# Top-2 experts computed on tokens that are sorted by expert on the chip

## What is computed

```python
def reference(x, Wq, Wk, Wv, w_gate, w_in, w_out):
    xn = _layernorm(x, axis=-1)
    # attention: Q, K, V = (xn @ W.T).reshape(H, b, s, 16)
    #   out = softmax(Q K^T) V, y = out + xn, normalised over each batch entry
    logits = xn @ w_gate.T
    top_logits, top_idx = jax.lax.top_k(logits, 2)
    top_gates = softmax(top_logits)
    gates = (one_hot(top_idx, 8) * top_gates[..., None]).sum(axis=1)
    for e in range(8):
        y = y + gates[:, e:e + 1] * ((xn @ w_in[e].T) @ w_out[e].T)
    return x + attention + y
```

## Time and profile before

| | us |
|---|---|
| median of 3 runs | 1054.75 |
| lowest, highest | 1052.57, 1057.66 |
| the profiled execution | 1050.42 |
| its span in the trace | 1048.6 |
| busy: TensorE, VectorE, ScalarE, GpSimd | 1007.0, 875.9, 627.5, 78.4 |

### The profile page before, as it was taken

One profiled execution on the slowest core, in us unless ns is written; L12 is line 12 of the kernel. 1 busy time (PEld: TensorE's weight loads), 2 busy tenths in 40 slices (PEclk: granted clock), 3 DMA queues, 4 the chain that ended last, 5 costly groups with the idle time before them and its releaser, 6 DMA issues.

```text
span 1048.6 us, 20711 instructions
## 1 busy us (share of the span) xinstructions
PE 1007.0 (96%) x7816; PEld 524.0 (50%) x7816; DVE 875.9 (84%) x1255; ACT 627.5 (60%) x1231; POOL 78.4 (7%) x205
## 2 busy tenths in 40 slices
PE   6698999999999999999999999999999999999995
PEld 6476788888885433333333333333333333333332
DVE  4331678787768999999999999999999999999976
ACT  2120011211110288888888888888888888888885
POOL 2100011001100000000000000000000000010001
PEclk9899999999999899999999999999999999999998
DMA  9588346545555012222222222222222222222204
GB/s 349 212 290 265 101 107 170 151 122 165 145 147 159 5 54 73 60 72 58 72 60 72 60 70 62 70 62 68 64 68 64 63 69 64 68 61 70 61 27 161
DMA packets 127042, 108.58 MB, mean 104 GB/s; under 512 B 81120, under 2 KB 102368, under 8 KB 126944
## 3 DMA queue, kind: packets, MB, share of 16 engines
q1 hardware_dynamic: 114016, 86.03, 28.9%
q10 hardware_dynamic: 12928, 21.24, 6.0%
HBM read 80.75 MB, written 42.21 MB: 117 GB/s over the span
## 4 chain that ended last, share of the span: by engine, by line
PE 89%; DVE 6%; issue 1%; DMA 1%; ACT 1%; ACTq 1%; POOL 0%; SPq 0%; POOLq 0%; DVEq 0%
PE ps L921 27%; PE ps L903 22%; PE ps L856 15%; PE ps L891 11%; PE ps L819 5%; PE ps L792 3%; PE ps L807 2%; PE ps L932 2%; DVE negm L628 1%; PE ps L944 1%; DVE acc L616 1%; PE ps L780 1%; ACTq L443 1%; DVE spare L560 1%; ACT stage L440 1%
## 5 line engine op out<-in xcount | busy, mean ns | idle before, releaser
L628 DVE TENSOR_REDUCE negm<-ps 128x1 f32<-128x1024 f32 x512 | 619.0, 1222 | 30.4 <-PE ps L891 12.1
L472 ACT ACTIVATE wp<-ps 128x512 f32<-128x512 f32 x684 | 369.4, 603 | 87.3 <-PE ps L903 60.1
L903 PE MATMUL ps<-qf,kf 50*128 50x512 f32 x1024 | 388.6, 456 | 1.9 <-DVE ps L696 1.7
L891 PE MATMUL ps<-kf,qf 48*128 48x512 f32 x1024 | 368.2, 450 | 0.2 <-DVE negm L628 0.2
L903 PEld LDWEIGHTS ps<-qf,kf 50*128 50x128 f32 x1024 | 160.0, 186 | 206.4 <-ACT wp L472 107.3
L921 PE MATMUL ps<-wp,vb 128*17 128x256 f32 x2736 | 215.4, 387 | 0.3 <-issue 0.3
L891 PEld LDWEIGHTS ps<-kf,qf 48*128 48x128 f32 x1024 | 145.9, 186 | 7.4 <-issue 5.7
L472 ACT ACTIVATE vstage<-ps 128x512 f32<-128x512 f32 x170 | 102.4, 602 | 24.9 <-PE ps L903 11.2
L856 PE MATMUL ps<-mth,xth 128*128 128x512 f32 x256 | 103.8, 405 | 3.4 <-DVE spare L560 2.5
L921 PEld LDWEIGHTS ps<-wp,vb 128*17 128x17 f32 x2736 | 46.9, 95 | 119.1 <-ACT wp L472 45.9
L472 ACT ACTIVATE picks<-ps 128x512 f32<-128x512 f32 x170 | 102.6, 603 | 0.0
(11 more groups left out here) (106 smaller groups left out, 724.0 us busy)
## 6 DMA issues: line engine op xcount, KB each, us to landing
feat_d<-qk_d SPq DMA_DIRECT2D x64, 256.0 KB, 4.4
qf<-feat_d SPq DMA_DIRECT2D x128, 128.0 KB
qk_d<-stage ACTq DMA_DIRECT2D x32, 256.0 KB
qk_d<-spare ACTq DMA_DIRECT2D x32, 256.0 KB
qf<-feat_d SPq DMA_DIRECT2D x128, 64.0 KB
kf<-feat_d SPq DMA_DIRECT2D x128, 64.0 KB
v_d<-vstage ACTq DMA_DIRECT2D x8, 544.0 KB, 4.9
vb<-v_d SPq DMA_DIRECT2D x128, 34.0 KB, 2.6
```

Of the source, the lines that this page charges most:

```text
L472: nc.scalar.activation(weight_tile(n, j, b)[:, h * HALF:(h + 1) * HALF], ps[:, ST_BANK[(2 * unit + b) % 3], :], ACT.Exp).then_inc(exp_done, 1)
L628: nc.vector.tensor_reduce(negm[:, n % 2, qt:qt + 1], ps[:, b:b + 2, :].rearrange("p b c -> p (b c)"), AX.X, ALU.max, negate=True).then_inc ...
L891: last = nc.tensor.matmul(ps[:, MAX_BANK[turn % 2] + half, :], qf[rows, u, qt * P:(qt + 1) * P], kf[rows, u, :], start=True, stop=True)
L903: nc.tensor.matmul(ps[:, ST_BANK[(2 * unit + half) % 3], :], kf[rows, u, j * P:(j + 1) * P], qf[rows, u, h * HALF:(h + 1) * HALF], start=T ...
```

## The change

Each token is computed with its two experts only. The 32 tiles are two parts of 16 (`PARTS`, `PT`). VectorE counts the choices (`count_choices`), TensorE makes running counts over partitions (`rank_choices`, three small matmuls), and VectorE works out at which tile each expert's tokens start (`start_tiles`), the row of each token and choice (`place_choices`) and the expert of each of 40 tiles (`name_owners`). GpSimd scatters the layernormed tokens by indirect DMAs of 128 rows into a table in HBM (`xs_d`), which SP has cleared whole by one plain DMA for each part. The sorted table has room for 40 tiles a part (each expert's rows filled up to a tile), so 80 tiles or 20 blocks of four are computed whatever the choices. A block is loaded (`sorted_tokens`), transposed, split and multiplied (`expert_tile`): high and low half of the expert's matrix stand side by side in `mm`, so the four matmuls give high x both (512 columns) and low x high (256), twice. The expert's number is read from registers. ScalarE copies the second half of the bank (`expert_out`), VectorE adds the first (`add_halves`), SP stores the block (`expert_rows`). In stage C GpSimd gathers each token's two rows, weights and adds them (`gather`, `combine`).

What moves with it: the projections of chunks 2 to 7 stand alone before the sorted products; the first 16 score maxima stand behind blocks 4 to 19; 48 of the 64 regroups move into stage C; weights have three slots, since `xn` is written by the layernorm itself; the layernorms of stage A are earlier.

```diff
+    AHEAD = 16
+    PARTS = 2
+    PT = NT // PARTS
+    MOST = PT * P // P
+    TILES = -(-((2 * PT * P + E * (P - 1)) // P) // TC) * TC
+    MB = TILES // TC
+    NMB = PARTS * MB
+    PACK = 8
+    WORDS = TILES // PACK
+    WARM = NMB - 2 * NKT
...
+    xs_d = [nc.dram_tensor(f"xs_d{i}", [TILES * P, D], FP32, kind="Internal").ap() for i in range(PARTS)]
+    ys_d = [nc.dram_tensor(f"ys_d{i}", [TILES * P, D], FP32, kind="Internal").ap() for i in range(PARTS)]
...
-        room = [wp[:, i, :] for i in range(4)] + [xn[:, TC * c:TC * (c + 1), :].rearrange("p t d -> p (t d)") for c in range(NC // 2, NC)]
+        room = [wp[:, i, :] for i in range(4)] + [xnc[:, i].rearrange("p t d -> p (t d)") for i in range(2)]
         win = [r.rearrange("p (h d) -> p h d", h=HU) for r in room[0::2]]
         wout = [r.rearrange("p (h d) -> p h d", h=HU) for r in room[1::2]]
         WS = len(win)
...
+                i = 2 * e + s
+                slot, earlier = i % WS, i - WS
                 if earlier >= 0:
-                    sp.wait_ge(*((m_ready, KT * (earlier + 1)) if s else (half_done, earlier + 1)))
+                    sp.wait_ge(*((m_ready, KT * (earlier // 2 + 1)) if earlier % 2 else (half_done, earlier // 2 + 1)))
...
+            sp.wait_ge(att_const, 2)
+            for part in range(PARTS):
+                sp.dma_start(xs_d[part].rearrange("(p r s) d -> p r (s d)", p=P, s=2),
+                             ot[:].rearrange("p g b t -> p (g b t)")[:, 0:2 * D].unsqueeze(1).to_broadcast([P, TILES // 2, 2 * D])
+                             ).then_inc(cleared[part], 16)
...
+            def sorted_tokens(b):
+                if b >= 2:
+                    sp.wait_ge(xt_psum, KT * (NC + b - 1))
+                if b % MB == 0:
+                    sp.wait_ge(scattered[b // MB], 16 * 2 * PT)
+                sp.dma_start(xnc[:, b % 2], xs_d[b // MB][b % MB * CH:(b % MB + 1) * CH].rearrange("(t p) d -> p t d", p=P)).then_inc(xs_in[b % 2], 16)
+
+            def expert_rows(b):
+                sp.wait_ge(moe_added, TC * (b + 1))
+                sp.dma_start(ys_d[b // MB][b % MB * CH:(b % MB + 1) * CH].rearrange("(t p) d -> p t d", p=P), outs[b % 4]).then_inc(ys_out[b % 4], 16)
+
+            sp.wait_ge(m_ready, KT * E)
+            sorted_tokens(0)
+            sorted_tokens(1)
+            for b in range(NMB):
+                if b >= 1 and b + 1 < NMB:
+                    sorted_tokens(b + 1)
+                if b == NMB - 2:
+                    max_rows(0)
+                expert_rows(b)
 
             for n in range(NB - 1):
                 if n:
                     sp.wait_ge(pv_done, NKT * n)
                 values(n + 1)
                 max_rows(n + 1)
+                if n + AHEAD < NB:
+                    regroup(n + AHEAD)
...
+            for part in range(PARTS):
+                pool.wait_ge(cleared[part], 16)
+                for k in range(2):
+                    pool.wait_ge(placed, 2 * part + k + 1)
+                    for t in range(PT * part, PT * (part + 1)):
+                        nc.gpsimd.indirect_dma_start(
+                            out=xs_d[part], out_offset=bass.IndirectOffsetOnAxis(ap=placeu[:, k, t:t + 1], axis=0),
+                            in_=xn[:, t, :], in_offset=None).then_inc(scattered[part], 16)
+            def gather(t):
+                part = t // PT
+                if t == 0:
+                    pool.wait_ge(xt_psum, KT * (NC + NMB))
+                if t % PT == 0:
+                    for i in range(4):
+                        pool.wait_ge(ys_out[i], 16 * len(range(i, MB * (part + 1), 4)))
+                for k in range(2):
+                    nc.gpsimd.indirect_dma_start(
+                        out=xnc[:, t % 2, k, :], out_offset=None, in_=ys_d[part],
+                        in_offset=bass.IndirectOffsetOnAxis(ap=placeu[:, k, t:t + 1], axis=0)).then_inc(gathered[t % 2], 16)
+
+            def combine(t):
+                rows = xnc[:, t % 2, 0:2]
+                pool.wait_ge(gathered[t % 2], 32 * (t // 2 + 1))
+                nc.gpsimd.tensor_tensor(rows, rows, gates[:, t, :].unsqueeze(2).to_broadcast([P, 2, D]), ALU.mult
+                                        ).then_inc(weighted, 1)
+                pool.wait_ge(weighted, 2 * t + 1)
+                nc.gpsimd.tensor_tensor(xnc[:, t % 2, 0], xnc[:, t % 2, 0], xnc[:, t % 2, 1], ALU.add).then_inc(weighted, 1)
+                pool.wait_ge(weighted, 2 * t + 2)
+                nc.gpsimd.tensor_tensor(acc[:, t, :], acc[:, t, :], xnc[:, t % 2, 0], ALU.add).then_inc(acc_done, 1)
...
+            for n in range(NB):
                 if n % 2 == 0 and n >= 4:
                     residual(n // 2 - 2)
                 max_halves(n)
+                if n % 2:
+                    gather(n // 2)
+                elif n:
+                    combine(n // 2 - 1)
+            combine(NT - 1)
...
+            xt_out(2)
             for c in range(2, NC):
-                xt_out(c)
                 v_out(c)
-                second_weight(c)
+                if c + 1 < NC:
+                    xt_out(c + 1)
+                if c > 2:
+                    second_weight(c - 1)
                 qk_out(c)
+            second_weight(NC - 1)
+
+            def expert_out(i):
+                b, t = divmod(i, TC)
+                if b >= 4 and t == 0:
+                    act.wait_ge(ys_out[b % 4], 16 * (b // 4))
+                act.wait_ge(moe_ready, i + 1)
+                nc.scalar.copy(outs[b % 4][:, t, :], ps[:, Y_BANK[i % 4], D:2 * D]).then_inc(moe_half, 1)
+
+            xt_out(NC)
+            for half in range(2):
+                act.wait_ge(qk_stored[half], 64 * NC)
+            for i in range(PARTS * TILES):
+                expert_out(i)
+                if i % TC == 0 and i + TC < PARTS * TILES:
+                    xt_out(NC + i // TC + 1)
+            act.wait_ge(named, PARTS)
...
+            def count_choices(c):
+                rows, own = slice(TC * c, TC * (c + 1)), TC * c % PT
+                g(nc.vector.tensor_tensor(occ[:, own:own + TC], oh1[:, rows], oh2[:, rows], ALU.add))
+                for t in range(own, own + TC):
+                    dve.wait_ge(summed, TC * c + t - own)
+                    nc.vector.tensor_tensor(before[:, t + 1], before[:, t], occ[:, t], ALU.add).then_inc(summed, 1)
...
+            def place_choices(part):
+                rows = slice(PT * part, PT * (part + 1))
+                own = work[:, 0:PT * E].rearrange("p (t e) -> p t e", e=E)
+                for k, onehot in enumerate((oh1, oh2)):
+                    g(nc.vector.tensor_tensor(own, place, onehot[:, rows], ALU.mult))
+                    g(nc.vector.reduce_sum(placef, own, AX.X))
+                    nc.vector.tensor_scalar(placeu[:, k, rows], placef, float(P), None, ALU.mult).then_inc(placed, 1)
+                    dve.wait_ge(placed, 2 * part + k + 1)
...
+            def add_halves(i):
+                b, t = divmod(i, TC)
+                dve.wait_ge(moe_half, i + 1)
+                nc.vector.tensor_tensor(outs[b % 4][:, t, :], ps[:, Y_BANK[i % 4], 0:D], outs[b % 4][:, t, :], ALU.add
+                                        ).then_inc(moe_added, 1)
...
             m_lo(0)
-            dve.wait_ge(const_step, 6 + E)
+            layernorm(1)
+            dve.wait_ge(const_step, CONSTS)
+            dve.wait_ge(ones_done, 2)
             choose_experts(0)
             m_lo(1)
             dve.wait_ge(w_lo, 2)
             qk_lo_halves(0, range(4))
+            lo_halves(1)
             gate_weights(0)
-            layernorm(1)
-            lo_halves(1)
+            count_choices(0)
...
+            lo_halves(2)
+            layernorm(NC - 1)
+            for c in range(2, NC):
+                if c > 2:
+                    choose_experts(c - 1)
+                    count_choices(c - 1)
+                if c + 1 < NC:
+                    lo_halves(c + 1)
+                if c == NC // PARTS:
+                    start_tiles(0)
+                qk_lo_halves(c, range(2))
+                if c == NC // PARTS:
+                    place_choices(0)
+                qk_lo_halves(c, range(2, 4))
+                if c > 2:
+                    gate_weights(c - 1)
+                if c == NC // PARTS + 1:
+                    name_owners(0)
+
+            choose_experts(NC - 1)
+            count_choices(NC - 1)
+            gate_weights(NC - 1)
+            start_tiles(1)
+            place_choices(1)
+            name_owners(1)
+            lo_halves(NC)
+            for i in range(PARTS * TILES):
+                add_halves(i)
+                if i % TC == 0 and i + TC < PARTS * TILES:
+                    lo_halves(NC + i // TC + 1)
+                if i == PARTS * TILES - 1:
+                    dve.wait_ge(moe_added, PARTS * TILES)
                     nc.vector.memset(ps[:, PV_BANK, 0:POS // 4 + P], 0.0).then_inc(att_const, 1)
-                maxima(n, qt)
-                if n == 1 and qt == 1:
```

(42 more changed lines are left out.)

274 lines of the change are left out of this document (132 added, 142 removed).

## The result

The changed kernel takes **1195.76 us** (1192.38 to 1199.79) where the one before, run beside it, takes 1054.4 us: a ratio of 1.134, 95% interval 1.129 to 1.138. The profiled execution has a span of 1193.0 us. Forecast was 1102 us, range 1060 to 1145: the sign was right, the size not. The loss against the kernel before is 141 us where some 50 were forecast.

What follows compares the result with a forecast made beforehand. TensorE was taken to bound the expert stage alone, and attention with ScalarE and VectorE close behind. Profiled 1050.4 us, plus 50 for a later first attention score, plus 2 in attention, gave 1102 us; range 1060 to 1145.

Steps and rivals of the forecast that it cites:

- Stage A: Weights and expert matrices, before the first token-by-expert product: end forecast at 96 us (94 to 106) instead of 105.65.
- Projections at 12.9 us a chunk, ScalarE's pace: Chunks 2 to 7 without dense products as cover: ScalarE's copies and DMA issues set 12.9 us each, 77 for six.
- only the stores of a chunk must land within its round: Bare projections: the argument against DMA saturation, whose cost was put at 4 us more per chunk.
- 112 us of work in 108 us of time: DMA from about 90 us on: clearings, stores, scatter, regroups and features, lasting until 202 us or later.
- saturation rival: Bare projections: chunk stores land late, each of six chunks takes 4 us longer, 1126 us in all; chance 0.13.
- VectorE's list after the last projection: Before the first sorted tile: 48 small operations and two low halves, 13 us uncovered on TensorE; tile at 198 us.
- GpSimd's writes: Scatter into the sorted table: 32 issues at 1.3 us from about 142 us, done at 184, so not late.
- Blocks at 10.8 us: Sorted experts: each block of four tiles holds one whole DMA trip, 10.8 us (8.5 to 13.2).
- half of 3.0 us: Sorted blocks: transposes and three tiles at 1.2 GHz would cost 3.0 us more; 1.5 us was taken.
- Attention +2: Attention stage: regroups and gathers hidden, but more traffic beside the row maxima's transfer, 2 us longer (0 to 30).
- The sign: Whole kernel: slower than before, with chance 0.88.
- the blocks' load trip: Sorted blocks: next load issued only behind the previous block's store, landing in 4.7 us (3.9 to 5.4), exposed each block.

Runs made afterwards that it cites:

- the ladder: Chunks 2 to 7, one thing added per step: forecast 72.5 us, stores and work alone 76.2, attention's preparation 94.3, clearings 111.6, indirect writes 129.4.
- x3: Changed kernel without GpSimd's indirect writes and without the two table clearings, blocks loading the input instead: 1141.8 us.
- x4: Changed kernel with each sorted block's load issued one block earlier, ahead of a store: 1096.0 us, ratio 1.042 to the kernel before.
- x12: x4 with spaced indirect writes, regroupings paced or moved behind blocks, features ahead of the first block, maxima's rows first in attention: 1075.6 us, ratio 1.020.
- x6: x4 with a GpSimd memset of 1024 columns ahead of each indirect write, to space them: 1087.5 us, ratio 1.029.

## Why the prediction was wrong

- **Stage A**: right in its direction. The last product of two weights ended at 92.4 us, below the bounds of 94 to 106, and the first value product came 4.7 us earlier than forecast. The gap ahead of expert 5's products, which was to grow from 3.87 us to 5.3, fell to 2.58.
- **Projections at 12.9 us a chunk, ScalarE's pace**: this step failed: 57 us over, of which 5 were kept in hand for DMA (198 to 203) and 4.7 came back from stage A; the rest is the 48 us of the first tile. By the ladder the 57 are 4 for the work and the stores themselves, 18 for the attention's preparation, 17 for the clearings and 18 for the indirect writes. ScalarE's own terms nearly hold when it is alone (13.8 to 15.4 us a chunk), but one of them, 0.59 us for the issue of a store, was too small here: the 40 issues of chunks 2 to 6 took 37.2 us instead of 24. The wait that I let off with "only the stores of a chunk must land within its round" is what failed: they didn't land within it, and one was waited for 17.3 us. DMA was priced by bytes, as 112 us of work in 108 us of time; x3 shows a store waited for while only 2.1 of sixteen engines are busy, which a price by bytes over all of them can't hold. The saturation rival had the place and the mechanism, and sized it at 24 us; it was 35 by the two steps of the ladder.
- **VectorE's list after the last projection**: right; from the last chunk's first value copy to the first tile 25.5 us, forecast 12.9 + 13.
- **GpSimd's writes**: 1.3 us each was right (1.27), their end at 184 near (192.3, from 151.8 instead of 142). What failed is that I asked only when they end and put what they do to others at nothing: 39 us in all, 12 by traffic, 27 by form, 13 of them ahead of the first tile and 25 in the first blocks. No row of before could show it, and none of the rivals had it.
- **Blocks at 10.8 us**: right, 11.2. The loads landed in 4.7 us as taken. Of the clock I had taken half of 3.0 us; the transposes took 1.97 us in every block, where 0.87 is the length at the full clock, and the three tiles 2.5 to 3.9 instead of 2.1; together that is 2.2 us over the full clock in the mean. By that the Trainium skill, "TensorE: Matmul & The Clock Gate", section "HAM oscillation", which lets every round of such a loop start at the low clock, was nearer than my half. 18 x 0.4 = 7 us; the other 25 of the 33 us lost in the blocks are the second stall.
- **Attention +2**: measured +13.8, inside its bounds of 0 to 30. The cause I named, more traffic beside the row maxima, was it, and mis-sized: 11.5 us are the reads.
- **The sign**: the blocks' load trip, which was to decide it, is there and cost 94 us. But slower would have come out without it too: x4, where the trip is hidden, is still 42 us over before, by the terms that I had wrong.

**Left open**: why ScalarE's waits for TensorE take so long beside dense indirect writes, even where the work waited for was done before. The runs show that both form and density are needed, not the mechanism; the trace puts part of the waits down to an unknown queue and the others to nothing that it sees. Loading of code hardly explains it: from 150 to 200 us the profile has three packets of the instruction queues, 0.3% of the DMA engines' time.

## What to carry to other kernels

When a long TensorE phase is removed, its cover goes for every transfer that stood beside it: price each store that gates a buffer with all that is queued in its stretch, ask how many of the DMA engines each transfer keeps busy and not only its bytes, and ask what total is left. Issue the load of the next round ahead of the store of this one. Before issuing indirect DMAs in a dense row, measure what they do to the waits of other engines, not only when they are done.

## What the runs showed of the hardware

- 32 indirect writes of 128 rows, one each 1.27 us, went with single waits of ScalarE of 7 to 13 us in the first part and 4 to 10 us in the second; the same bytes by plain DMAs every 0.54 us did not, nor indirect ones every 1.7 us (x12) or 2.1 us (x6).
- A store of 256 KB was waited for 20.9 us (x3, from 115.18), and for 7 of them (125.5 to 132.5) the DMA share was 0.13, 2.1 of sixteen engines.
- ScalarE's issue of such a store took 0.59 us when little was queued and up to 4.96 us (x3, at 110.18) beside the features and stores of that stretch.
